# Gate and up weights of each expert loaded as two DMAs of 64 partitions instead of one of 128

## Chip, cores and metric

The kernel runs on one core of one Trainium2 chip. The metric is the device time of one execution in microseconds (us). Three executions of the kernel before took 776.88, 773.20 and 776.39 us; their median, 776.39 us, is the time before. Every row below comes from one profiled execution, which took 775.46 us; its first to its last instruction, the span, took 773.7 us.

## The reference

The program is a small vision tower in float32: 16 images become 16 x 37 = 592 tokens of 256 features. A patch embedding with two layernorms is followed by one attention block with rotary positions, a mixture of experts, six encoder layers, and a gated feed-forward whose operands are rounded to 4-bit floats in blocks of 16. The change touches the weights of the mixture alone:

```python
C = int(T * F_C / E)                                  # 592 * 2 / 16 = 74 tokens an expert
scores = jax.nn.softmax(flat_x @ gate_w.T, axis=-1).T # 16 experts x 592 tokens
topk_weight, topk_idx = jax.lax.top_k(scores, C)
xg = flat_x[topk_idx]                                 # 16 x 74 x 256
g = jnp.einsum('ecd,eid->eci', xg, Wg)                # Wg: 16 x 1024 x 256
u = jnp.einsum('ecd,eid->eci', xg, Wu)                # Wu: 16 x 1024 x 256
h = jax.nn.gelu(g, approximate=False) * u
eo = jnp.einsum('eci,edi->ecd', h, Wd)                # Wd: 16 x 256 x 1024
eo = eo * topk_weight[..., None]
flat_out = jnp.zeros_like(flat_x).at[topk_idx.reshape(-1)].add(eo.reshape(-1, d))
```

## The kernel before

Features lie on the 128 partitions, in two chunks of 128, and tokens along the free dimension. The engines run programs of their own that meet at semaphores. SyncE (SP) issues every DMA, all on one queue, in the order of its program.

In the mixture all 16 experts are computed one after the other. An expert's weights lie in memory as 128 rows, one for each partition, of 6144 float32: first the gate and up weights (4096 values, 16 KB of a row, 2048 KB in all), then the down weights (2048 values, 8 KB of a row, 1024 KB in all). They are loaded into a ring of three places (`ERING = 3`): `GU[s]` holds gate and up weights, `DOWN[s]` down weights, `s` being the expert's number modulo 3. Two of the places lie in the big tensor that the profile calls `arena`; the third is `GU_THIRD` with a piece of `LW`. A third, small load for each expert, the route (L672), copies a row of 592 token positions to 80 partitions; the matmuls that scatter the expert's result use it.

TensorE's program (`expert_step`) does for each expert n: the gate matmuls of expert n+1 (64 matmuls, L1199), the down matmuls of expert n (64, L1230), the up matmuls of expert n+1 (64, L1199), the scatter of expert n-1 (8, L1246) and two transposes (L1238). Expert numbers run from 0 to 15. The gate matmuls wait at L1190 for `ld_gu[s]`, the semaphore of the gate/up load into that place.

SyncE's program before the loop issues the gate/up and down loads of experts 0 and 1, five loads of the feed-forward's weights (`QW`), and the gate/up load of expert 2. Then it stores the token positions to memory (L690), waits until they have landed, and issues three routes, expert 2's down load and three loads for the first encoder layer (the last of them, 1024 KB, is `w1`). After that `load_ahead(k, n)` runs for k = 1 to 13. It waits until the up matmuls of expert k-1 are done, issues the gate/up load of expert k+2, then (from k = 2 on) a route, waits until the down matmuls of expert k-1 are done and issues the down load of expert k+2. For k = 1 there is no route; for k = 2 to 13 this is a hardware loop of four rounds with three experts each.

A DMA adds 16 to its semaphore when it has landed, and each place of the ring has a semaphore of its own, so L1190 waits for 16 times the number of loads into that place.

Of the kernel before, what the change touches and what calls it, by code (L numbers as in the profile page):

```python
# [24 lines left out]
P = 128  # L25
# [64 lines left out]
EGU_N = 2 * C * EI  # L90
# [66 lines left out]
def build(nc, a):  # L157
# [8 lines left out]
    with ExitStack() as ctx:  # L166
# [3 lines left out]
        def sem(name):  # L170
            return ctx.enter_context(nc.semaphore(name))
# [135 lines left out]
        GU = [EW[0][:, 0:EGU_N], EW[1][:, 0:EGU_N], GU_THIRD[:, :]]  # L307
# [133 lines left out]
        ld_gu, ld_down, ld_route = ([sem(f"{n}{s}") for s in range(ERING)] for n in ("ld_gu", "ld_down", "ld_route"))  # L441
# [198 lines left out]
        def _(sp):  # L640
# [21 lines left out]
                sp.dma_start(LW[:, lo:lo + n], a["lw"][l][:, lo:lo + n]).then_inc(s, 16)  # L662

            def load_gate_up(e, s):
                sp.dma_start(GU[s], a["ew"][e][:, 0:EGU_N]).then_inc(ld_gu[s], 16)

            def load_down(e, s):
                sp.dma_start(DOWN[s], a["ew"][e][:, EGU_N:EW_N]).then_inc(ld_down[s], 16)
# [6 lines left out]
            for s in range(2):  # L675
                load_gate_up(s, s)
                load_down(s, s)
# [8 lines left out]

            sp.wait_ge(u_ready, 2)
            load_gate_up(2, 2)
            sp.wait_ge(pos_cast, 1)
            sp.dma_start(pos_store, pos16[0:E, 0:N]).then_inc(route_stored, 16)  # L690
# [10 lines left out]
            def load_ahead(k, n):  # L701

                sp.wait_ge(u_psum, k * 2)
                load_gate_up(k + 2, (n + 2) % ERING)
                if not isinstance(k, int):
                    sp.wait_ge(shot_ready, k - 1)
                    load_route(k + 1, (n + 1) % ERING)
                sp.wait_ge(d_psum, k)
                load_down(k + 2, (n + 2) % ERING)
# [40 lines left out]
        def _(pe):  # L750
# [435 lines left out]
            def expert_up(e, u):  # L1186

                s = e[1] % ERING
                if u == 0:
                    pe.wait_ge(ld_gu[s], turn_of(e) * 16 + 16)  # L1190
                    pe.wait_ge(xg_staged, idx(e) + 1)
                w = GU[s][:, u * C * EI:(u + 1) * C * EI].rearrange("p (c n) -> p c n", c=C)
                for half in range(2):
                    o = bank[2 * u + half]
                    for m in range(4):
                        for kc in range(C):
                            for lo in range(0, P, COL_TILE):
                                at = (4 * half + m) * P + lo
                                last = mm(o[lo:lo + COL_TILE, m * CAP:(m + 1) * CAP], w[:, kc, at:at + COL_TILE],  # L1199
                                          XGS[:, s, kc, :], start=(kc == 0), stop=(kc == C - 1))  # L1200
                    last.then_inc(g_psum if u == 0 else u_psum, 1)

            def idx(e):

                return e[0] * ERING + e[1]

            def turn_of(e):

                return e[0] + e[1] // ERING
# [40 lines left out]
            def expert_step(i, n):  # L1250

                nxt = (i, n + 1)
                gate_free(nxt)
                expert_up(nxt, 0)
                expert_down((i, n))
                up_free(nxt)
                expert_up(nxt, 1)
                if n > 0:
                    expert_scatter((i, n - 1))
                turn_output((i, n))  # L1260

            pe.wait_ge(moe_act, MOE_ACT["xg7"])
            expert_up((0, 0), 0)
            pe.wait_ge(score_out, 1)
            expert_up((0, 0), 1)
# [1788 lines left out]
```

## Time and profile before

| What | Value |
|---|---|
| Median of three executions | 776.39 us |
| Profiled execution, whole | 775.46 us |
| Its span | 773.7 us |
| TensorE busy (matmul) | 749.2 us, 97% |
| VectorE busy | 553.2 us, 72% |
| ScalarE busy | 426.0 us, 55% |
| GpSimd busy | 247.5 us, 32% |
| Moved by DMA | 83.91 MB, mean 108 GB/s |
| Gate/up loads | 16 of 2048 KB |
| Mean granted TensorE clock | 0.996 of full |

A busy share is an average over stages with different limits. The expert stage runs from about 129 us to 266 us of the span; what bounds it is read from its own stretch. In the page's second part each digit or number stands for one of 40 slices of 19.3 us, so slices 8 to 13 are the expert stage.

### The profile page before, as it was taken

The page shows a single profiled execution, that of the slowest core. Times are in us where ns is not written, and L with a number is a line of the kernel's source. Part 1 is how long each engine was busy: PE and PEld are TensorE (multiplying, and loading weights), DVE is VectorE, ACT ScalarE, POOL GpSimd, SP SyncE. Part 2 cuts the span into 40 slices and gives each one's busy share as a digit, 9 for nine tenths or more (in the row PEclk, how much of TensorE's full clock was granted, in tenths as well). Part 3 has the DMA queues.
Part 4 walks back from the last instruction along what each step waited for, and adds up shares of the span by engine and source line. Part 5 has one row for each costly group of instructions (what it writes and reads, how often), then busy time and mean ns, then how long its engine had stood idle before and what let it go on. Part 6 is the DMA issues. An engine that isn't in the chain of part 4 may idle for free.

```text
span 773.7 us, 19820 instructions
## 1 busy us (share of the span) xinstructions
PE 749.2 (97%) x7780; PEld 693.6 (90%) x7780; DVE 553.2 (72%) x1209; ACT 426.0 (55%) x816; POOL 247.5 (32%) x299
## 2 busy tenths in 40 slices
PE   9999999899999999999999999999999999999988
PEld 8898779789999898989999999989998998988758
DVE  6797592345444487787978788887978787776896
ACT  3387422222222366767876786778678677835421
POOL 0002130211111004633661474256246614633020
PEclk9999999899999999999999999999999999999999
DMA  6000765989997120103100310111031003300001
GB/s 202 1 24 33 328 250 192 373 319 392 390 414 282 56 113 1 43 15 108 42 0 14 108 41 14 54 54 41 14 108 41 0 14 109 114 1 1 1 1 32
DMA packets 16732, 83.91 MB, mean 108 GB/s; under 512 B 2848, under 2 KB 8496, under 8 KB 10672
## 3 DMA queue, kind: packets, MB, share of 16 engines
q1 hardware_dynamic: 16688, 83.30, 29.0%
q8 instruction: 31, 0.51, 0.3%
q14 instruction: 13, 0.11, 0.0%
HBM read 80.50 MB, written 2.79 MB: 108 GB/s over the span
## 4 chain that ended last, share of the span: by engine, by line
PE 44%; issue 25%; POOL 19%; DVE 9%; ACT 3%; POOLq 0%; DVEq 0%; ACTq 0%
PE bank L1199 9%; POOL W_L L2083 7%; PE bank L1230 4%; POOL HF_L L2141 4%; POOL arena L2059 4%; PE bank L757 3%; PE bank L1246 3%; POOL WQKV_L L2083 3%; PE bank L909 2%; PE bank L1087 2%; PE bank L782 2%; PE bank L942 2%; PE bank L825 1%; POOL SQ L2102 1%; PE bank L1179 1%
## 5 line engine op out<-in xcount | busy, mean ns | idle before, releaser
L2059 POOL TENSOR_TENSOR arena<-arena,srec 111x456 f32<-111x456 f32 x56 | 52.3, 962 | 120.0 <-DVE srec L2237 120.0
L2083 POOL TENSOR_TENSOR W_L<-LW,W_H 128x256 fp32r<-128x256 f32 x96 | 68.5, 750 | 35.4 <-DVE XHL L2659 32.0
L2141 POOL TENSOR_TENSOR HF_L<-arena,HF_H 128x296 fp32r<-128x296 f32 x48 | 43.8, 934 | 75.7 <-ACT HF_H L1974 75.7
L825 PE MATMUL bank<-XHL,W_H 128*128 128x296 f32 x288 | 64.8, 306 | 0.0
L1974 ACT ACTIVATE arena<-bank,vec 128x296 f32<-128x296 f32 x96 | 48.8, 509 | 20.8 <-PE bank L825 15.1
L1397 PE MATMUL bank<-HF_L,W_H 128*128 128x296 f32 x192 | 57.4, 299 | 0.0
L1397 PE MATMUL bank<-HF_H,W_H 128*128 128x296 f32 x192 | 57.4, 299 | 0.0
L1397 PE MATMUL bank<-HF_H,W_L 128*128 128x296 f32 x192 | 57.3, 299 | 0.0
L909 PE MATMUL bank<-arena 114*128 114x111 f32 x448 | 55.1, 276 | 0.8 <-issue 0.6
L909 PEld LDWEIGHTS bank<-arena 114*128 114x128 f32 x448 | 53.1, 192 | 2.6 <-issue 1.3
L2249 DVE TENSOR_SCALAR OB<-bank,lvec 96x148 f32<-96x148 f32 x144 | 50.8, 366 | 5.7 <-PE bank L909 3.3
L878 PEld LDWEIGHTS bank<-arena 128*111 128x111 f32 x448 | 52.3, 175 | 1.1
L878 PE MATMUL bank<-arena 128*111 128x114 f32 x448 | 52.7, 260 | 0.0
L1199 PE MATMUL bank<-XGS,arena 128*64 128x74 f32 x1408 | 51.4, 232 | 1.4 <-issue 1.4
L1199 PEld LDWEIGHTS bank<-XGS,arena 128*64 128x64 f32 x1408 | 48.6, 139 | 3.7 <-issue 3.4
L2233 DVE TENSOR_REDUCE ssum<-arena 111x12 f32<-111x456 f32 x56 | 32.1, 608 | 23.8 <-ACT arena L1613 23.7
L1974 ACT ACTIVATE HF_H<-bank,vec 128x296 fp32r<-128x296 f32 x96 | 48.3, 503 | 0.0
L825 PEld LDWEIGHTS bank<-XHL,W_H 128*128 128x128 f32 x288 | 48.2, 188 | 0.0
L2095 POOL TENSOR_TENSOR QW<-QW,arena x14 | 17.9, 1277 | 94.2 <-DVE QW L2576 58.0
L825 PE MATMUL bank<-XHL,WQKV_H 128*128 128x296 f32 x192 | 45.4, 311 | 0.0
L2102 POOL TENSOR_TENSOR SQ<-SQ 128x296 f32<-128x296 f32 x24 | 19.6, 816 | 79.4 <-ACT SQ L1601 79.4
L757 PE MATMUL bank<-ones_d 128*128 128x128 f32 x324 | 43.4, 286 | 1.4 <-DVE U L2263 1.4
(286 smaller groups left out, 2052.6 us busy)
## 6 DMA issues: line engine op xcount, KB each, us to landing
arena<-ew_in SPq DMA_DIRECT2D x11, 2048.0 KB, 10.3
LW<-lw_in SPq DMA_DIRECT2D x12, 1024.0 KB, 4.9
arena<-ew_in SPq DMA_DIRECT2D x11, 1024.0 KB, 7.5
GU_THIRD<-ew_in SPq DMA_DIRECT2D x5, 2048.0 KB, 10.4
LW<-ew_in SPq DMA_DIRECT2D x5, 1024.0 KB, 6.1
LW<-lw_in SPq DMA_DIRECT2D x6, 768.0 KB, 4.4
fp_weights<-arena SPq DMA_DIRECT2D x1, 2048.0 KB, 6.4
arena<-fp_weights SPq DMA_DIRECT2D x1, 2048.0 KB, 7.2
```

The costliest lines, as they stand in the source:

```text
L757: mm(o[:, SPARE_AT:SPARE_AT + P], ones_d[:, :], ones_d[:, :], start=alone, stop=alone, skip_group_check=True)
L825: last = mm(o, w, x, start=(i == 0), stop=(i == len(pairs) - 1))
L878: last = mm(o[0:QROWS, col:col + KROWS], Qe[:, h, c, bb].rearrange("p s q -> p (s q)"), Ke[:, at_half(plan, h), c, bb].rearrange("p g k -> ...
L909: last = mm(o[:, i * QROWS:(i + 1) * QROWS], Ve[0:KROWS, at_half(plan, h) * HB + b % HB, c * P:(c + 1) * P], PTr[0:KROWS, b % PSLOTS, c, : ...
L1199: last = mm(o[lo:lo + COL_TILE, m * CAP:(m + 1) * CAP], w[:, kc, at:at + COL_TILE], XGS[:, s, kc, :], start=(kc == 0), stop=(kc == C - 1))
L1397: last = mm(bank_of(plan, keys[c])[:, 0:NHALF], w, moving, start=(m == 0 and i == 0), stop=(m == FM - 1 and i == 2))
L1974: last = f(out[:, m, :], bank_of(plan, ("f1", FM * hy + m))[:, 0:NHALF], ACT.Gelu, bias=vec[:, 3 * C + m:3 * C + m + 1])
L2059: nc.gpsimd.tensor_tensor(v, v, srec[0:QROWS, s:s + 2, :].unsqueeze(3).to_broadcast([QROWS, 2, C * JH, KEYS]), ALU.mult).then_inc(p_ready, 1)
L2083: last = nc.gpsimd.tensor_tensor(low[:, cols], value[:, cols], high[:, cols], ALU.subtract)
L2141: nc.gpsimd.tensor_tensor(HF_L[:, m, :], HF[:, m, :], HF_H[:, m, :], ALU.subtract).then_inc(hl_ready_pool, 1)
L2233: v.tensor_reduce(pair_view(ssum, p), pair_probs(p), AX.X, ALU.add).then_inc(s_sum, 1)
L2249: return v.tensor_scalar(dst, src, bias(c)[lo:hi, :], None, ALU.add)
```

## The change

`load_gate_up` issues two DMAs, one for partitions 0 to 63 and one for partitions 64 to 127, each with its 16 KB of every row: the same bytes, to the same place, on the same queue. Both add to the same semaphore, so a whole load adds 32, and the matmuls wait for 32 times the number of loads instead of 16 times.

```diff
             def load_gate_up(e, s):
-                sp.dma_start(GU[s], a["ew"][e][:, 0:EGU_N]).then_inc(ld_gu[s], 16)
+                for lo in range(0, P, P // 2):
+                    rows = slice(lo, lo + P // 2)
+                    sp.dma_start(GU[s][rows, :], a["ew"][e][rows, 0:EGU_N]).then_inc(ld_gu[s], 16)
...
                 s = e[1] % ERING
                 if u == 0:
-                    pe.wait_ge(ld_gu[s], turn_of(e) * 16 + 16)
+                    pe.wait_ge(ld_gu[s], turn_of(e) * 32 + 32)
                     pe.wait_ge(xg_staged, idx(e) + 1)
```

On SyncE, the rows of the kernel before in the first third of its loop over the experts (`arena<-ew_in` of 128x4096 is a gate/up load, of 128x2048 a down load; `u_psum` and `d_psum` count finished up and down matmuls, `shot_ready` counts scatter matrices built by VectorE):

```order
L665 ISA [waits u_psum]
L665 DMA arena<-ew_in 128x4096
L706 REGISTER_ALU
L672 ISA [waits shot_ready]
L672 DMA arena<-positions 80x592
L668 ISA [waits d_psum]
L668 DMA arena<-ew_in 128x2048
L703 REGISTER_ALU
```

The same place in the changed kernel, whose lines stand two further down:

```order
L667 ISA [waits u_psum]
L667 DMA arena<-ew_in 64x4096
L667 ISA
L667 DMA arena<-ew_in 64x4096
L708 REGISTER_ALU
L674 ISA [waits shot_ready]
L674 DMA arena<-positions 80x592
L670 ISA [waits d_psum]
L670 DMA arena<-ew_in 128x2048
L705 REGISTER_ALU
```

One DMA of 128 rows has become two of 64 rows, with one register instruction between them. The order of everything else, and every wait on SyncE, is as it was; on the other engines no instruction is added or moved.

## Rows read from the trace of the kernel before

**Rows 1.** The page, second part: granted clock and DMA share by slice.

```profile
PEclk9999999899999999999999999999999999999999
DMA  6000765989997120103100310111031003300001
```

**Rows 2.** Chain of waits, expert stage: start us, us, what.

```profile
146.46 2.94 issue
...
153.05 3.79 PE bank L1199 x64
...
167.66 1.39 issue
...
179.82 2.22 PE bank L1199 x64
...
187.68 2.22 PE bank L1199 x64
...
250.62 2.22 PE bank L1199 x64
```

**Rows 3.** DMA issues: out<-in, engine, count, KB each, median us to landing.

```profile
arena<-ew_in SPq DMA_DIRECT2D x11, 2048.0 KB, 10.3
...
arena<-fp_weights SPq DMA_DIRECT2D x1, 2048.0 KB, 7.2
...
arena<-fp_weights SPq DMA_DIRECT2D x1, 64.0 KB, 7.6
positions<-arena SPq DMA_DIRECT2D x1, 18.5 KB, 1.5
```

**Rows 4.** Timeline of SyncE's queue: start us, us of issue, engine, line.

```profile
98.19 0.63 SPq L665 DMA_DIRECT2D GU_THIRD<-ew_in  x1
...
113.23 0.37 SPq L690 DMA_DIRECT2D positions<-arena  x1
...
116.97 1.12 SPq L662 DMA_DIRECT2D LW<-lw_in  x2
133.20 0.33 SPq L665 DMA_DIRECT2D arena<-ew_in  x1
...
170.64 0.34 SPq L665 DMA_DIRECT2D arena<-ew_in  x1
...
233.56 0.33 SPq L665 DMA_DIRECT2D arena<-ew_in  x1
```

**Rows 5.** Line 665, the load issued at 170.64 us.

```profile
DMA to landing us min/median/max: 8.6/8.6/8.6
```

**Rows 6.** Line 665, the load issued at 233.56 us.

```profile
DMA to landing us min/median/max: 11.0/11.0/11.0
```

**Rows 7.** Windows: stretch and length, busy by engine, granted clock, DMA share, GB/s.

```profile
136.00:139.00 3.00, 3.00 (x100) 3.00 (x97) 0.14 (x1) 1.35 (x4) 0.00 (x0) 1.00 1.01 431
...
149.40:153.00 3.60, 3.60 (x23) 2.98 (x22) 0.46 (x1) 0.00 (x0) 0.00 (x0) 0.51 0.97 340
153.00:156.80 3.80, 3.80 (x69) 3.80 (x70) 2.88 (x6) 0.89 (x2) 0.00 (x0) 0.56 0.98 410
...
176.00:240.00 64.00, 64.00 (x1656) 61.52 (x1654) 31.17 (x65) 15.00 (x42) 10.83 (x9) 1.00 1.01 398
...
245.50:245.75 0.25, 0.25 (x14) 0.25 (x12) 0.21 (x2) 0.00 (x0) 0.00 (x0) 1.00 0.63 244
...
247.00:247.25 0.25, 0.25 (x14) 0.25 (x12) 0.00 (x0) 0.16 (x1) 0.25 (x1) 1.00 0.07 24
```

**Rows 8.** Line 665, the load issued at 98.19 us.

```profile
DMA to landing us min/median/max: 13.3/13.3/13.3
```

**Rows 9.** Line 662, the two loads issued from 116.97 us.

```profile
DMA to landing us min/median/max: 7.3/8.3/9.3
```

**Rows 10.** Timeline of ScalarE: start us, us, line, output, input.

```profile
138.16 1.47 ACT L1852 ACTIVATE WQKV_H<-LW 128x1536 fp32r<-128x1536 f32 x1
```

**Rows 11.** Timeline of VectorE, columns as in rows 10.

```profile
142.06 0.80 DVE L2564 TENSOR_REDUCE arena<-QW  x1
```

## Prediction

> **What bounds the kernel now.** I read the slices first. The granted clock is near full throughout, and the DMA engines are idle in most of the span, except in slices 8 to 12, about 140 to 240 us, where their share is 8 or 9 tenths [rows 1]. That is the expert stage, the only stretch where the touched loads matter, so I asked next for its chain of waits. It is TensorE all the way: an expert's step starts at 179.82 us and the next at 187.68, so a step is 7.86 us, and no piece of the chain is a wait for a transfer. There are two gaps, of 2.94 and 1.39 us, put down to issue [rows 2]. TensorE sets the pace, then, and the loads are hidden. How well are they hidden? That needs the queue's timeline, the landing times of single loads, and windows of DMA traffic.
>
> The gate/up load issued at 170.64 us lands after 8.6 us; the one issued at 233.56, eight steps later, after 11.0 [rows 4 to 6]. The landing time grows by 2.4 / 8 = 0.30 us a step, so the DMA engines need 7.86 + 0.30 = 8.16 us for the loads of one step. Bytes agree: 2048 + 1024 + 92.5 KB are 3.24 MB, and at the 398 GB/s of the stretch 176 to 240 us 8.14 us, and the DMA share there is 1.01 [rows 3, 7]; the 92.5 KB, the route, are 80 rows of 592 two-byte values. The stage has two resources that are almost in balance, and the DMA side is already the slower one. It is covered only by a head start: the load of expert 15 lands at 233.56 + 11.0 = 244.56 us and its gate matmuls start at 250.62 [rows 2], so 6.06 us are to spare at the last expert.
>
> **The change part by part.**
>
> *Issue.* Each load needs one more DMA issue (0.33 us [rows 4]) and a register instruction. There are 16 loads, 13 of them from 133.2 us on. SyncE does nothing but issue and wait here, and queued behind the second half are a route and a down load, each 0.4 us later. With 6 us to spare for the loads this costs nothing on the path. The wait on TensorE is the same instruction with another constant.
>
> *The transfer.* The bytes are the same. The question is whether a transfer to half of the partitions moves at the full rate. The trace has no large one. Bounds from both sides: at the rate of the whole stage nothing changes, and a load takes 2.097 MB / 398 GB/s = 5.27 us of the engines' time. The nearest row with 64 partitions is the 64 KB reload of the feed-forward's weights, issued about 0.4 us behind a 2048 KB one on 128 partitions. They land after 7.6 and 7.2 us [rows 3], so the small one ends about 0.8 us later; 65.5 KB in 0.8 us are 82 GB/s, and a whole load at that rate would take 25.6 us. That end is far too dear, since a small transfer is mostly fixed time, but it shows nothing that speaks for full rate. Between 82 and the best rate seen, 431 GB/s [rows 7], the geometric mean is 188. I take the simplest case near it: half the partitions, half the rate, because the engines then share half of the ways into the memory. The ways that are left are never idle then, so I halve the best rate: 215 GB/s, 9.73 us a load. The two halves follow each other in each engine's queue, so a second half starts only when an engine has done its part of the first; where engines are apart in time, both sides of the memory are in use for a while. At the end of the queue the share falls to 0.63 at 245.5 and 0.07 at 247.0 us [rows 7]: the engines finish over some 1.5 us, so they are apart by a fraction of a microsecond. I take off 0.4 and use 9.3 us.
>
> The Trainium skill has a rule on just this (SBUF — State Buffer, Door 1: The DMA port swizzle): partitions 0 to 63 reach 8 of 16 ports, as 64 to 127 do, measured there at 196 GB/s against 328 for all 128. Its section "Can I just issue two DMAs to hit both halves?" says no, "they serialize", at +6% over one. By that a load would take 2.097 MB / 208 GB/s = 10.1 us, as an estimate, and the sum below would end some 11 us higher, near 832. No row here shows a large transfer of 64 partitions, so neither the rule nor its rate is tested by this trace.
>
> *Sum.* The other loads of a step take 8.16 - 5.27 = 2.89 us, so the DMA engines need 9.3 + 2.9 = 12.2 us a step against 7.86 on TensorE. The spare time is gone after two or three experts, and from then on TensorE waits for each load. Two gate/up loads are always outstanding (the ring has three places), so the engines never run dry and the last landing is a plain sum:
> - Start. The three front loads grow by 3 x (9.3 - 5.3) = 12 us. Expert 2's, issued at 98.19, landed at 111.5 [rows 4, 8]; now 123.5. The store of positions, issued at 113.23, stands behind it in each queue and lands near 124.5, not 113.23 + 1.5 = 114.7 [rows 3, 4]. SyncE waits for it, so what follows is 9.8 us late. The last of it, `w1`, issued by 117.6 with 9.3 us to landing, ended at 126.9 [rows 4, 9], now at 136.7. Expert 3's load, issued at 133.20, gets going at about 136.3.
> - 13 gate/up loads (experts 3 to 15) x 9.3 = 120.9.
> - 12 down loads and 12 routes ahead of the last one, 12 x 2.9 = 34.8.
> - Landing after the last byte: 0.5.
>
> 136.3 + 120.9 + 34.8 + 0.5 = 292.5 us, where the gate matmuls of expert 15 started at 250.62: 41.9 us later. Their remaining work follows as before, but for the clock. After the gap of 2.94 us the granted clock was 0.51 and 0.56 for the next 7.4 us, that is 1.2 GHz in place of 2.4, and 64 gate matmuls took 3.79 us instead of 2.22 [rows 2, 7]. The waits now are longer, 12.2 - 7.86 = 4.3 us each. Inside the stage a slow stretch only eats into the next wait. After the last load it counts once: 7.4 x (1 - 0.54) = 3.4 us. In all 41.9 + 3.4 = 45.3, on the profiled 775.46: 820.8, so 821 us. The median shown is 0.9 us above the profiled run, which I leave out.
>
> *What follows late.* The front loads' delay has cover: the first encoder weights are read by ScalarE from 138.16 us [rows 10], and the last of them is there by 136.7; the feed-forward weights, issued ahead of expert 2's load, are read by VectorE from 142.06 [rows 11] and land before it, so before 123.5. Nothing there is added. After the stage the program is the same.
>
> **The rivals.**
>
> *Hidden anyway (chance 0.12).* If a half costs only a fixed 0.8 us more, as the small row has it, a load takes 6.1 us. The last landing must stay under 250.6: (250.6 - 133.2 - 0.5 - 34.8) / 13 = 6.3 us a load is the point from which the change decides anything. Up to a load 19% slower the time stays 775 to 776, and no change is seen. Against it: the spare 6 us shrink already now by 0.3 a step.
>
> *In part (0.10).* Engines far enough apart, or a rate limited elsewhere, at 7.5 us a load: 134.2 + 97.5 + 34.8 + 0.5 = 267.0, which is 16 us late, some 792 us with little clock loss. For it: engines did finish over 1.5 us. Against: a lead is not increased by sharing, it needs chance.
>
> *Slow clock throughout (0.10).* If the waits keep the clock at 1.2 GHz, a step of TensorE is 7.86 x 3.79 / 2.22 = 13.4 us, more than the DMA's 12.2. From 153 us, 12.5 steps x 5.5 us are 69 us: 845. Against: such a step has no wait, and the clock rose after 7.4 busy us. The rates worse than half stand here too.
>
> *Faster (0.04).* The two issue gaps lie beside full DMA engines. If they are TensorE's own code arriving late behind 128-row transfers, and halves let it through sooner, up to 2.94 + 1.39 + 3.4 of clock = 7.7 us go: 768. It decides only if loads stay under 6.3 us. Against: the code's packets would meet as many bytes in front of them.
>
> *That it doesn't do what it says:* the order shows two DMAs of 64x4096 for each load, so this is out.
>
> **How the numbers follow.** The forecast, half rate, has 0.64, with a range of its own from 808 (8.3 us a load) to 836 (10.5, half of 398 GB/s). Reaching up to most of the slow clock case and down over the partial one gives 784 to 852, which leaves out hidden, faster and the extreme ends, about 2 in 10. A measurement of this kernel can tell 0.5%, 3.9 us, from no change. Faster by more: 0.04. Within: 0.11 (nearly all of hidden). Slower: 0.85.
>
> **What would show it.** In the profile after: gate/up landings (the later half) that grow from about 12 us to 25 or more; DMA rate in the stage near 3.24 MB / 12.2 us = 266 GB/s with the share still at 1; gate matmuls of line 1199 waiting for `ew_in` in front of each expert from 5 or 6 on, some 4 us each or less with a slow clock; the granted clock falling in slices 8 to 14; a stage ending about 45 us later and nothing else changed. If the rate stays near 398 GB/s and landings at 9 to 11 us, the step on the transfer is wrong and the time is that of before. If loads are slow and the time is not, the ring covers more than I worked out.

## The result and the profile after

Six executions of the changed kernel took 846.8 to 859.2 us, median 849.9; six of the kernel before 772.1 to 776.9, median 775.9. The medians lie 74.0 us apart, and the ratio is 1.100, with a 95% interval of 1.097 to 1.103. The forecast was 45 us slower, 821 us. The profiled execution took 852.4 us, its span 850.6, which is 76.9 us more than before. Where four executions of a kernel spread by more than 1.5% (e2_middle, e3_quarters and e6_front_whole below), its ratio is taken from the two fastest alone, while ranges and medians are of all four.

The page after, second part, answers to [rows 1]: granted clock, then DMA share and GB/s in 40 slices, now of 21.3 us each.

```profile
PEclk9999999889878878999999999999999999999999
DMA  5012998999999992201021012002102101120001
GB/s 183 1 50 57 222 245 255 233 220 236 225 239 227 245 240 83 102 1 39 13 99 37 12 49 83 3 12 99 37 12 99 37 12 58 42 104 1 1 1 30
```

Where the expert loads run, slices 5 to 15, the DMA share reads 8 or 9 tenths, as it did at its fullest before, but the engines move 220 to 255 GB/s. The two stretches of 64 us that answer to the 398 GB/s of [rows 7] (busy time by engine, then granted clock, DMA share, GB/s):

```profile
176.00:240.00 64.00, 46.03 (x944) 43.82 (x940) 19.37 (x40) 8.64 (x24) 5.46 (x5) 0.83 1.01 231
240.00:304.00 64.00, 45.54 (x918) 44.05 (x920) 15.91 (x33) 8.08 (x22) 6.38 (x5) 0.77 1.01 234
```

The share is 1.01 in both kernels, the rate has gone from 398 GB/s to between 231 and 234. TensorE, busy for all 64 us before, is busy for 46. The chain of waits, which had no transfer in it before [rows 2], now runs through the second halves of gate/up loads (start us, us, what):

```profile
188.30 22.28 DMA arena<-ew_in
...
210.81 3.91 PE bank L1201 x64
...
219.73 35.14 DMA arena<-ew_in
...
255.13 3.95 PE bank L1201 x64
...
264.09 33.72 DMA arena<-ew_in
...
298.07 4.22 PE bank L1201 x64
...
311.56 4.22 PE bank L1201 x64
...
321.91 2.95 issue
324.86 4.24 PE bank L1201 x63
```

The last gate group, of expert 15, starts at 324.86 us instead of 250.62 [rows 2]: 74.2 of the 76.9 us. The piece called issue ahead of it is a wait too: the second half of that load was issued at 293.7 us and landed after 31.0, at 324.7. The gate groups shown take 3.9 to 4.2 us where they took 2.2. Each follows a wait and runs with a granted clock near one half, 1.2 GHz (0.50 in 324 to 328 us, shown further down). Landing times of the two halves, for the loads issued from 219 and from 293 us, answer to [rows 5, 6]; the matmuls need both, so the max counts:

```profile
DMA to landing us min/median/max: 29.0/32.1/35.1
```

```profile
DMA to landing us min/median/max: 22.8/26.9/31.0
```

Outside the stage little moved: from 343 us on the busy times of all engines are within 1% of those that the old kernel shows from 267. In 80 to 129 us, where the front loads run, the busy times are the same too and the rate fell from 298 to 228 GB/s.

### The profile page after: what moved, and what is told of

It is laid out like the page before. It is cut to its first block, busy times and chain, and to the rows that moved or that the text cites. A ratio compares the mean times of both kernels' runs of the same rounds, so it can differ in the third digit from the quotient of the medians.

```text
span 850.6 us, 19868 instructions
## 1 busy us (share of the span) xinstructions
PE 775.9 (91%) x7780; PEld 719.1 (85%) x7780; DVE 553.2 (65%) x1209; ACT 426.1 (50%) x816; POOL 247.5 (29%) x299
## 4 chain that ended last, share of the span: by engine, by line
PE 35%; issue 25%; POOL 17%; DMA 11%; DVE 8%; ACT 3%; POOLq 0%; SPq 0%; DVEq 0%; ACTq 0%
DMA arena<-ew_in 11%; PE bank L1201 7%; POOL W_L L2085 7%; POOL HF_L L2143 4%; POOL arena L2061 3%; PE bank L1232 3%; PE bank L759 3%; POOL WQKV_L L2085 2%; PE bank L911 2%; PE bank L1089 2%; PE bank L784 1%; PE bank L944 1%; POOL SQ L2104 1%; PE bank L1181 1%; PE bank L1559 1%
## 5 line engine op out<-in xcount | busy, mean ns | idle before, releaser
L1201 PE MATMUL bank<-XGS,arena 128*64 128x74 f32 x1408 | 64.8, 263 | 31.6 <-DMA arena<-ew_in 20.7
L2586 DVE TENSOR_TENSOR arena<-arena,bank 128x296 f32<-128x296 f32 x32 | 14.7, 461 | 117.7 <-PE bank L1201 117.7
L1201 PEld LDWEIGHTS bank<-XGS,arena 128*64 128x64 f32 x1408 | 61.5, 168 | 34.5 <-issue 34.2
L1976 ACT ACTIVATE arena<-bank,vec 128x296 f32<-128x296 f32 x96 | 48.9, 509 | 20.8 <-PE bank L827 15.1
L1836 ACT ACTIVATE arena<-bank 128x296 f32<-128x296 f32 x32 | 13.3, 417 | 85.6 <-PE bank L1201 85.6
L1201 PE MATMUL bank<-XGS,GU_THIRD 128*64 128x74 f32 x640 | 30.5, 267 | 19.3 <-DMA GU_THIRD<-ew_in 9.8
```

Of the source, the lines that this page charges most:

```text
L1976: last = f(out[:, m, :], bank_of(plan, ("f1", FM * hy + m))[:, 0:NHALF], ACT.Gelu, bias=vec[:, 3 * C + m:3 * C + m + 1])
```

## Experiments

### The rates by themselves, and columns instead of partitions

**m1_rates.** A new program of DMAs alone, from the same weights to the same partitions, in eleven stretches of six experts each (like m2_route and m3_ring further down, it ran once). A part of it:

```diff
+            phase([(0, 128, 0, EGU_N)])
+            phase([(0, 64, 0, EGU_N), (64, 128, 0, EGU_N)])
+            phase([(0, 128, 0, EGU_N // 2), (0, 128, EGU_N // 2, EGU_N)])
+            phase([(0, 64, 0, EGU_N)])
+            phase([(32, 96, 0, EGU_N)])
...
+            phase([(0, 64, 0, EGU_N), (64, 128, 0, EGU_N), (0, 128, EGU_N, EW_N)])
+            phase([(0, 64, 0, EW_N), (64, 128, 0, EW_N)])
```

> This program leaves out the whole computation: it only moves six experts' weights from memory to the 128 partitions, in eleven stretches that each wait for the one before, so that the DMA rate of each form can be read from windows. Theory S (sides): partitions 0 to 63 and 64 to 127 are reached over different ways, and a transfer to one side moves at half the rate whatever its partition count. Theory N (number): a transfer to fewer partitions is slower in proportion to their number, wherever they lie. Theory O (overhead): the cost is per DMA, not per way. Rates in GB/s, in order: (1) whole gate/up loads, all theories 400. (2) halves 0-63, 64-127 in turn: S 200 to 215, N 200, O near 350. (3) two DMAs of 128 partitions, each half of the columns: S and N 400, O near 350. (4) only 0-63: S and N 200, O 350. (5) only partitions 32-95, which is 64 partitions on both sides: S 400, N 200, O 350. (6) quarters 0-31, 64-95, 32-63, 96-127: S 215 or somewhat more, N 100, O 280. (7) 32-95, then 0-31, then 96-127: S 280, N 130, O 300. (8) whole gate/up and whole down in turn: 400. (9) halves of gate/up with a whole down: S 260 by a plain sum, 230 if the down loads are slowed too, as in the changed kernel. (10) gate/up and down together in halves: S 215. (11) the two halves issued from two queues at once: S 215 if both queues run through the same engines in step, up to 400 if they spread.

One window from the middle of each stretch, in the order of the expectation (only GpSimd's column, the clock, DMA share and GB/s are there):

```profile
10.00:20.00 10.00, 0.00 (x0) 1.00 1.00 429
50.00:60.00 10.00, 0.00 (x0) 1.00 1.01 215
110.00:120.00 10.00, 0.00 (x0) 1.00 1.02 424
140.00:150.00 10.00, 0.00 (x0) 1.00 0.99 202
165.00:175.00 10.00, 0.00 (x0) 1.00 1.01 431
200.00:210.00 10.00, 0.00 (x0) 1.00 1.04 228
260.00:270.00 10.00, 0.00 (x0) 1.00 1.02 247
310.00:320.00 10.00, 0.00 (x0) 1.00 1.02 433
390.00:400.00 10.00, 0.00 (x0) 1.00 1.04 256
460.00:470.00 10.00, 0.00 (x0) 1.00 0.98 204
520.00:560.00 40.00, 0.00 (x0) 1.00 1.01 227
```

Halves run at half of the whole, 215 against 429. It is not the number of DMAs (two column halves: 424), and not the number of partitions: 64 partitions from 32 to 95 run at 431. It is which partitions they are, theory S. The last window is the one with two issuing queues: 227. A window of 10 us is good to some 3%: over 40 us of their stretches halves read 213 and quarters 221.

By the Trainium skill (SBUF — State Buffer, Door 1: The DMA port swizzle), partitions 0 to 63 reach 8 of 16 ports, and its table of ports gives 32 to 95 all 16. These rows agree. Its rates for single transfers of 1 MiB, 196 and 328 GB/s, lie below the 202 and 429 of these streams. Its section "Can I just issue two DMAs to hit both halves?" gives +6% for two over one, and here it is 215 against 202, also 6%.

**e1_columns.**

```diff
-                sp.dma_start(GU[s], a["ew"][e][:, 0:EGU_N]).then_inc(ld_gu[s], 16)
+                for lo in range(0, EGU_N, EGU_N // 2):
+                    cols = slice(lo, lo + EGU_N // 2)
+                    sp.dma_start(GU[s][:, cols], a["ew"][e][:, cols]).then_inc(ld_gu[s], 16)
```

> Each gate/up load is two DMAs of 128 partitions, each with half of the columns: as many DMAs, bytes and semaphore counts as in the changed kernel, but every transfer reaches all partitions. Theories S (sides) and N (number): as before, 774 to 778 us, landings 9 to 12 us, no wait of the gate matmuls for their weights. Theory O (overhead for each DMA): slower like the changed kernel, 850 us.

It took 774.6 us, ratio 0.999 (0.998 to 1.001). In its stretch 176 to 240 us it moves 387 GB/s:

```profile
176.00:240.00 64.00, 64.00 (x1652) 61.45 (x1648) 31.40 (x65) 14.49 (x40) 10.80 (x9) 1.00 1.01 387
```

The second issue, the second increment and the wait for 32 cost nothing that can be measured. The whole slowdown comes from the direction of the cut.

### Other cuts across the partitions

**e2_middle** and **e3_quarters**, in place of the two halves:

```diff
+                for lo, hi in ((32, 96), (0, 32), (96, 128)):        # e2_middle
...
+                for lo in (0, 64, 32, 96):                           # e3_quarters, 32 partitions each
```

> Each gate/up load is three DMAs: partitions 32 to 95 (64 partitions, both sides), then 0 to 31, then 96 to 127. Theory S (sides): the first at full rate, 2.6 us, the other two at half rate, 2 x 2.6 = 5.3 us or, at the price of the changed kernel (a step of 14.0 us, so 11.1 us for a load in halves), 5.5; a load takes 7.9 to 8.1 us and the last one lands about 20 to 25 us later than the start of its matmuls before: 795 to 803 us. Theory N (number): a load costs 5.3 + 2 x 5.3 = 16 us, above 880 us. Theory O: three DMAs, twice the extra of the changed kernel, above 900 us.

> Each gate/up load is four DMAs of 32 partitions, in the order 0-31, 64-95, 32-63, 96-127, so that the sides alternate every 512 KB instead of every 1024 KB. Theory S: still one side at a time if the engines run in step, 850 us; since engines that are apart by 1 us now reach both sides for a larger part of the time, 810 to 850 us. Theory N: a load at a quarter of the rate, 21 us, about 1000 us. Theory O: three times the extra of the changed kernel, about 1000 us.

e2_middle took 813.6 to 830.8 us, ratio 1.066 (1.060 to 1.072); e3_quarters 839.0 to 857.9, ratio 1.086 (1.082 to 1.090). Three DMAs are faster than two, which only theory S allows. The size was off: even the fastest execution is 11 us above the 803 of the expectation. In m1_rates this mix ran at 247 GB/s, not at the 280 of my plain sum, and in the kernel's trace the loads of experts 3 to 15 land 11.2 us apart on average, where 10.8 to 11.0 were expected. The start was late too: expert 3's load landed at 151.5 us, where it landed at 140.6 before. In the kernel:

```profile
176.00:240.00 64.00, 51.93 (x1306) 49.27 (x1301) 24.12 (x50) 11.40 (x32) 7.67 (x6) 1.00 1.02 298
```

Alternating the sides four times a load instead of twice gave 228 GB/s against 215 alone. In the kernel the medians are 848.1 and 849.9 us, which within the spread of the executions (2%) is no difference.

### A dose: one place of the ring

**e4_one_place.**

```diff
+                n = 2 if s == 2 else 1
+                for lo in range(0, P, P // n):
```

> Only the loads into the third place of the ring (experts 2, 5, 8, 11, 14) are in halves, the others whole. Sides theory with the price of the changed kernel, 11.1 us for a load in halves: of the 13 loads from 133 us on, 4 x 11.1 + 9 x 5.27 + 34.8 = 126.6 us, the last landing near 261, 10 us after its matmuls started before; 785 to 789 us. With the plain half rate, 9.7 us: 780. Rival: the cost comes only when halves follow halves in the queue, or the spare 6 us cover one load in three: no change, 776.

It took 788.5 us, ratio 1.020 (1.015 to 1.025), at the upper end of the 785 to 789 expected. Its chain has the load in halves issued at 205.24 us as a link, and three experts later, at the next load in halves, a gap ahead of gate matmuls near half the clock:

```profile
205.94 17.69 DMA GU_THIRD<-ew_in
...
247.63 4.91 issue
252.54 4.03 PE bank L1202 x64
```

So halves cost time even where no halves follow them, and the head start covers a part. The time came out as expected, but the price did not. From expert 7 to 14 the loads land 7.9 to 8.1 us apart where whole, and 12.9 to 13.0 where in halves. That is 4.9 us more for a load in halves, 10.2 in all, nearer to the plain half rate (9.7) than to the 11.1 that I had taken from the changed kernel. The high price of the changed kernel does not come with every load in halves.

### Why 14 us a step and not 12.2

**m2_route** and **m3_ring** are again DMAs alone; six experts with and without the small route load, and sixteen experts through three places:

```diff
+            mixed(WHOLE, False)
+            mixed(WHOLE, True)
+            mixed(HALVES, False)
+            mixed(HALVES, True)
...
+            ring(WHOLE, True, WHOLE)
+            ring(HALVES, True, WHOLE)
+            ring(HALVES, False, WHOLE)
+            ring(HALVES, True, HALVES)
```

> Leaves out the whole computation; loads of six experts, each stretch waiting for the one before. It asks why a step of the changed kernel took 14.0 us where six loads in halves with whole down loads ran at 257 GB/s, which is 12.2 us for an expert. What the kernel has and the first program had not is the route, 1184 bytes to each of 80 partitions, issued between gate/up and down. Theory R (route): its many short rows cost the engines about 0.9 us beside whole loads (8.16 us a step against 7.26 at 433 GB/s) and more beside halves. Stretches, in us for each expert: (1) whole gate/up and down 7.3; (2) the same with a route 8.2 (R) or 7.5 (only its bytes count); (3) halves and down 12.2; (4) the same with a route: R 13 to 14, bytes only 12.5; (5) routes alone: R about 0.9 each, bytes only 0.25; (6) partitions 32-95 alone: 2.5 each, again at full rate; (7) 32-95, 0-31, 96-127 with route and down: 10.5 to 11.5; (8) quarters with route and down: 13 to 14.

m2_route, the first four stretches and the seventh, from first to last byte; a sixth of each is an expert's time:

```profile
2.00:47.00 45.00, 0.00 (x0) 1.00 0.98 413
49.00:98.50 49.50, 0.00 (x0) 1.00 0.99 392
100.00:176.50 76.50, 0.00 (x0) 1.00 0.99 247
178.50:257.50 79.00, 0.00 (x0) 1.00 1.00 246
...
286.00:350.00 64.00, 0.00 (x0) 1.00 1.00 304
```

These are 7.5, 8.3, 12.8, 13.2 and 10.7 us. The eighth stretch, quarters with route and down load, took 12.8. A route costs whole loads 0.8 us, as theory R says (8.3 is also the 8.16 of the prediction), but halves only 0.4. Halves with whole down loads are at 12.8 before any route, where the plain sum of the rates has 2.10 MB / 215 + 1.05 MB / 431 = 12.2.

> Leaves out the whole computation; 16 experts' loads through three places, each place loaded again when its last load has landed, so that up to three experts' loads are in the queue. Four stretches: (1) whole gate/up, route, whole down; (2) halves, route, whole down, as in the changed kernel; (3) the same without route; (4) halves of both and route. Before, six experts took 8.3, 13.1, 12.8 us each for the first three. Question: is the step of 14.0 us in the kernel from long queues in which the engines move apart (theory A), or from TensorE's side (theory C)? A: (2) takes 13.5 to 14.5 us an expert over 16, and its end shows engines finishing over several us, as 320 to 327 us in the changed kernel. C: (2) 13.1 us as before, engines finishing over 1.5 us. Stretch (4): 15 us.

```profile
2.00:133.00 131.00, 0.00 (x0) 1.00 0.99 394
134.00:344.00 210.00, 0.00 (x0) 1.00 1.01 246
345.00:550.00 205.00, 0.00 (x0) 1.00 1.00 245
554.50:795.00 240.50, 0.00 (x0) 1.00 1.01 216
```

These are 8.2, 13.1, 12.8 and 15.0 us an expert. The second stretch has the loads of the changed kernel, and its mean is what it was with six experts, the number that the expectation gave to theory C. Its steps are even as well: twelve of 13.0 to 13.2 us but for one of 14.0. The fourth has steps of 15.0. But within the third the steps are not even. On the queue's timeline (start us, us of issue) each issue waits for a place to be full:

```profile
439.69 1.10 SPq L69 DMA_DIRECT2D W<-ew_in  x2
...
454.29 1.10 SPq L69 DMA_DIRECT2D W<-ew_in  x2
...
468.95 1.10 SPq L69 DMA_DIRECT2D W<-ew_in  x2
...
507.91 1.10 SPq L69 DMA_DIRECT2D W<-ew_in  x2
...
520.56 1.10 SPq L69 DMA_DIRECT2D W<-ew_in  x2
```

Steps of the same loads, with no compute engine at work, begin at 12.8 us, grow to 14.6 and 14.7, and fall back to 12.7. So the pace of halves beside whole loads can wander up to the 14 of the changed kernel and beyond. It did not in the stretch that is most like the kernel, so the kernel's mean of 14.2 over twelve steps is not reproduced by DMAs alone.

**e8_down_halves** cuts the down loads too.

```diff
-                sp.dma_start(DOWN[s], a["ew"][e][:, EGU_N:EW_N]).then_inc(ld_down[s], 16)
+                for lo in range(0, P, P // 2):
+                    rows = slice(lo, lo + P // 2)
+                    sp.dma_start(DOWN[s][rows, :], a["ew"][e][rows, EGU_N:EW_N]).then_inc(ld_down[s], 16)
```

> The changed kernel with the down loads in halves too. By the plain sum a down load at half rate takes 2.4 us more, so 12 of them 29 us: about 878 us. Theory A (engines far apart): in the changed kernel one engine of a pair is often still in a half of a gate/up load while the other is in a down load, over the same way into the memory, so the whole down loads are already slowed and the step of 14.0 us is what all transfers at half rate cost (3.15 MB at 215 GB/s, 14.6 us, with the route 15): 855 to 865 us.

It took 866.1 us, ratio 1.117 (1.113 to 1.121), 16 us more than the changed kernel instead of 28, and moved 216 and 217 GB/s in its two 64-us windows. With all transfers in halves, kernel and bare DMAs agree: 216 GB/s in m3_ring's last stretch, and in both the steps are 15.0 us, to within 0.3. A step of the changed kernel took 14.2, so there the whole down loads save 0.8 us of the 2.4 that the plain sum gives them. That fits theory A, whose 855 to 865 it just misses.

### The clock, and the start

**e5_warm** and **e7_warm_short** put matmuls of constants ahead of the wait:

```diff
                 gate_free(nxt)
+                constant_products(bank[0], 40)                       # e7_warm_short: 22
```

> The changed kernel with 40 matmuls of constants (128x128, about 4.4 us at the full clock) ahead of each expert's wait for its gate weights, so that TensorE is busy while it waits. Theory D (the DMA engines set the pace, the slow clock counts only after the last load): 3 us faster than the changed kernel, 845 to 850 us. Theory C (the slow clock sets part of the pace): the granted clock stays at 1.00 and the time falls by 15 us or more, to 835 or below.

> The changed kernel with 22 matmuls of constants ahead of each expert's wait for its gate weights. The run with 40 took 8.93 us for them, twice what I had reckoned, so that TensorE's own step of 16.8 us set the pace; 22 take 4.9 us and make a step of 12.8 us at the full clock, below the 14.0 of the changed kernel. Theory D (DMA sets the pace, the slow clock counts only at the end): granted clock near 1.00 and 846 us, 3 to 4 us less than the changed kernel. Theory C (the slow clock sets part of the pace): 835 or less.

e5_warm took 908.1 us, ratio 1.172 (1.169 to 1.176). I had taken a constant product for 0.11 us; it has two instructions of that length, and its chain shows 8.93 us of them in each step of 16.8:

```profile
207.39 8.93 PE bank L759 x80
216.32 2.23 PE bank L1201 x64
```

TensorE set the pace there, so the run says nothing on the clock. e7_warm_short took 864.4 us, ratio 1.114 (1.107 to 1.121), with a mean granted clock of 0.99 where the changed kernel had 0.956. Theory C, which wanted 835 or less, falls: full clock in the stage bought nothing. The changed kernel's own windows say the same, for with a DMA share of 1.01 in both the engines were not kept waiting for an issue by a slow TensorE. Theory D, with 846, missed its number too. From 201 to 282 us TensorE takes steps of 12.8 us without a wait for a load, and then one link of 40.5 follows:

```profile
277.90 2.23 PE bank L1201 x64
...
282.20 2.10 PE bank L1201 x64
...
285.16 40.51 DMA GU_THIRD<-ew_in
325.72 4.21 PE bank L1201 x64
```

In 316 to 320 us its DMA engines moved 141 GB/s at a share of 0.98, less even than halves alone do. The transfers got slower: the loads land 13.3 us apart at first and 18.8 at the worst, and the last landed at 335.4 us, 10.7 later than in the changed kernel. Another 4.9 us are the last 22 products, which run from 336.35 to 341.26 us, after that load had landed.

**e6_front_whole** leaves the first three gate/up loads whole.

```diff
+                n = 1 if isinstance(e, int) and e < ERING else 2
+                for lo in range(0, P, P // n):
```

> The changed kernel, but the loads of experts 0, 1 and 2, issued from 80 us on, are whole; those of experts 3 to 15 are in halves. In the changed kernel the last encoder load of the front landed at 144.7 us instead of 126.9, so expert 3's load started about 10 us late. Theory: that start counts in full, since the engines never run dry afterwards: about 10 us faster than the changed kernel, 840 us. Rival: the front is covered by the spare time, no difference from the changed kernel, 850 us.

It took 840.8 to 859.7 us, ratio 1.090 (1.083 to 1.096), against 1.100 (1.097 to 1.103) for the changed kernel. The executions of both spread over 12 to 19 us, and the medians of all are 850.3 and 849.9, so a gain of 10 us is neither shown nor excluded. The trace, of its slowest execution, shows that the start did move: expert 3's load landed at 147.1 us, 7.4 earlier than in the changed kernel. The twelve steps behind it then took 15.4 us each instead of 14.2, growing to 18.2 at the end, which is more than the gain. The pace of the steps differs from one execution to the next by more than the gain that this experiment looks for.

## Why the prediction was right in direction and short in size

The forecast was 821 us in a range of 784 to 852, and the median of 849.9 lies at the very end of that range.

*What bounds the kernel* held: the stage had two resources in balance and the loads lived on a head start. e1_columns and e4_one_place both came out as that reading says.

*Issue and wait* at nothing was right, as e1_columns shows.

*The transfer* at half rate was right, and everything hangs on this step. It was in part luck, for its basis was a 64 KB row and a guess between 82 and 431 GB/s; 429 and 215 GB/s are now measured. The ways are tied to partitions 0 to 63 and 64 to 127; the form "half the partitions, half the rate" was wrong as a rule, as 32 to 95 show.

*What failed is the term of the sum for a load, 9.3 us, with the down load beside it at full rate.* The last two gate groups start at 311.56 and 324.86 us, 13.3 apart; over the stage it is more: expert 3's load landed 20.7 us after its second half was issued at 133.8, at 154.5, and expert 15's matmuls started 170 us later, 14.2 us for each of twelve steps. I had 12.2, so 24 us of the missing 32 are here. The 2.0 us of a step have three parts:
- 0.4 us is the amount that I took off because engines that are apart use both sides. Halves alone ran at 215 GB/s, 9.75 us a load, so there was nothing to take off.
- 0.5 us is the price of the mix. Halves, route and whole down load took 13.1 us in m3_ring's second stretch, where 9.75 + 2.9 is 12.6.
- 1.1 us, from 13.1 to 14.2, appears in the kernel and not in that stretch.

The sum also counts twelve routes ahead of the last load, and the queue of the kernel before has eleven there. That is under 1 us.

I also counted engines that are apart as a gain, and the runs speak for the opposite. The end of a queue shows how far apart they are, as the time from the fall of the DMA share to the last byte. Before, it was 1.5 us, the last two windows of [rows 7]. The changed kernel needs 7, from 320 us on:

```profile
320.00:324.00 4.00, 1.91 (x23) 1.53 (x18) 1.97 (x5) 0.47 (x1) 0.00 (x0) 0.94 0.29 85
324.00:328.00 4.00, 3.14 (x49) 3.17 (x51) 1.95 (x3) 0.42 (x1) 1.27 (x1) 0.50 0.07 23
```

These are the same ends, in this order, in m3_ring (second and third stretch), e8_down_halves, e6_front_whole and e7_warm_short. The table sets them beside the steps from one landing to the next (in m3_ring, from one issue to the next):

```profile
343.00:344.00 1.00, 0.00 (x0) 1.00 0.28 115
549.00:552.00 3.00, 0.00 (x0) 1.00 0.16 66
342.00:344.00 2.00, 2.00 (x47) 2.00 (x46) 0.00 (x0) 0.52 (x2) 0.00 (x0) 0.67 0.21 55
326.00:334.00 8.00, 1.81 (x30) 1.84 (x32) 1.46 (x2) 0.00 (x0) 1.28 (x1) 0.58 0.16 40
328.00:338.00 10.00, 10.00 (x187) 9.88 (x184) 2.03 (x5) 1.60 (x4) 0.00 (x0) 0.83 0.21 66
```

| Stretch | Steps, us | Engines end apart by, us |
|---|---|---|
| m3_ring, halves with route | 13.0 to 13.2, one 14.0 | under 1 |
| m3_ring, halves without route | 12.7 to 14.7 | 5 |
| changed kernel | 13.2 to 14.8 | 7 |
| e6_front_whole | 13.8 to 18.2 | 9 |
| e7_warm_short | 13.3 to 18.8, last 9.7 | 10 |
| e8_down_halves, all in halves | 14.9 to 15.1 | under 2 |

Where halves and whole loads are mixed, uneven and long steps and engines that end far apart come together. Where engines end together the steps are even. A load is landed when its slowest engine is done, so each wait of TensorE is for the last of them. That the distance between the engines is the cause of the long steps is argued, not shown, and what drives them apart stays open.

*Start.* Expert 3's load should have landed at 136.3 + 9.3 + 0.5 = 146.1 us and did at 154.5; this is the other 8 us. The mechanism was right: the positions' store, issued at 113.20 us, landed after 16.1 us behind expert 2's load, and SyncE issued the routes at 129.37 instead of 114.7. The front loads were mis-sized by the same price; expert 2's landed at 129.2, not 123.5. Whether this start counts in full is what e6_front_whole could not tell, since its steps were slower.

*The clock.* From expert 15's gate matmuls to the first add behind the stage it took 18.6 us (324.86 to 343.50), and 15.9 before (250.62 to 266.51): 2.7 us, where I had 3.4. Inside the stage the granted clock was 0.77 to 0.83 and cost nothing that e7_warm_short could give back. So the rival with the slow clock throughout, whose 845 us came nearest to the time, was near by chance: its cause did not hold.

The measured terms add up: 8.4 (start) and 24 (steps) above the 41.9 foreseen are the 74.2 by which the last gate group is late, to 0.1, and with 2.7 of clock they make 76.9, the whole difference of the spans. This is bookkeeping on one trace. It says where the time went, and not why a step took 14.2. "Hidden anyway", "in part" and "faster" are out: a load in halves takes 9.75 us at the least, 85% more than 5.27, where 19% more would have used up the head start.

## What to carry to other kernels

If a transfer must be cut, cut it along the columns, or so that each piece holds partitions of both sides, as 32 to 95 do; a cut at 64 halves the rate although every engine reads as fully busy. Read the GB/s beside the DMA share: a share of 1.0 stood beside 429, 215 and in one place 141 GB/s. And where hidden loads run at the rate of the compute, work out how much longer one may take before the head start is gone, here 19%, before touching its form.

## What the runs showed of the hardware

- 64 partitions from 32 to 95 load at 431 GB/s, 64 from 0 to 63 at 202 to 208, both in DMAs of 1024 KB with the same share of 1.0.
- Issuing the two sides from two queues at once gave 227 GB/s, as little help as quarters on one queue (228).
- A load of 1184 bytes to each of 80 partitions, 95 KB, costs 0.8 us beside whole loads (m2_route), and six of them alone ran at 74 GB/s.
- The pace of a steady stream of halves and whole loads wandered between 12.7 and 14.7 us an expert with no compute engine at work, and its engines ended 5 us apart. The same stream with a route between them stayed at 13.0 to 13.2 but for one step, and ended within 1 us.
- With every transfer in halves the loads landed 15.0 us apart, in the kernel and without it.
